# Order of the last eight units: where norms are chained and which engine scales them

## What is computed

```python
x = _layernorm(x + _L0_gnn_ref(x, adj, ...), axis=-1)
x = _layernorm(x + _L1_gnn_ref(x, adj, ...), axis=-1)
x = _layernorm(x + _L2_gnn_ref(x, adj, ...), axis=-1)
x = _layernorm(x + _L3_gnn_ref(x, adj, ...), axis=-1)
# layer 3, three times:
effects = einsum('nm,bmd->bnd', adj_matrix, v)
h = relu(concatenate([v, effects]) @ W1.T + b1)
v = h @ W2.T + b2
```

## Time and profile before

| | |
|---|---|
| median of 3 runs | 1065.37 us (1065.24 to 1068.3) |
| the profiled execution | 1068.64 us, of which the span from the first to the last instruction is 1066.8 us |
| TensorE (PE) busy | 1029.9 us, 97% of the span |
| VectorE (DVE) busy | 726.3 us, 68% |
| ScalarE (ACT) busy | 422.6 us, 40% |
| GpSimd (POOL) busy | 536.0 us, 50% |
| granted TensorE clock, mean | 0.991 of full speed |

### The profile page before, as it was taken

The page is one execution under the profiler, slowest core; times in us unless marked ns, Lnnn a source line. Parts: engine busy times, 40 slices in busy tenths (PEclk is TensorE's granted clock), DMA queues, the critical chain, the costliest instruction groups (busy, mean ns, idle before and its releaser), DMA issues.

```text
span 1066.8 us, 18773 instructions
## 1 busy us (share of the span) xinstructions
PE 1029.9 (97%) x6922; PEld 494.1 (46%) x6922; DVE 726.3 (68%) x1751; ACT 422.6 (40%) x1081; POOL 536.0 (50%) x623
## 2 busy tenths in 40 slices
PE   7979999999999999999999999999999999999994
PEld 3436444434443444344345555555554545455542
DVE  5855566577556776776674899988756776767556
ACT  3631233333434444434432564446345422132633
POOL 0001497645455866675682566677954232323310
PEclk9989999999999999999999999999999999999998
DMA  9760000000000000000010121212212100000022
GB/s 369 269 241 1 1 2 1 2 1 2 1 1 1 2 2 1 2 1 1 2 40 2 40 79 41 80 41 76 73 50 80 41 1 1 3 1 22 20 60 60
DMA packets 14658, 45.65 MB, mean 43 GB/s; under 512 B 961, under 2 KB 9281, under 8 KB 10081
## 3 DMA queue, kind: packets, MB, share of 16 engines
q1 hardware_dynamic: 14560, 44.39, 11.5%
HBM read 40.19 MB, written 4.19 MB: 42 GB/s over the span
## 4 chain that ended last, share of the span: by engine, by line
PE 82%; DVE 9%; DMA 2%; ACT 2%; POOL 2%; issue 1%; SPq 0%; POOLq 0%; ACTq 0%; DVEq 0%
PE PS L731 33%; PE PS L860 20%; PE PS L904 18%; DMA R<-at_in 2%; PE PS L716 2%; PE PS L718 2%; PE PS L717 2%; DVE T L1178 1%; DVE X L1178 1%; ACT T L1023 1%; PE PS L725 1%; PE PS L723 1%; PE PS L724 1%; DVE BW L1175 1%; DVE S L1178 1%
## 5 line engine op out<-in xcount | busy, mean ns | idle before, releaser
L731 PE MATMUL PS<-BW,S 128*128 128x512 fp8e4 x1792 | 405.2, 380 | 8.5 <-DVE T L1178 5.6
L731 PEld LDWEIGHTS PS<-BW,S 128*128 128x128 f16 x1792 | 170.0, 98 | 216.6 <-issue 18.0
L860 PE MATMUL PS<-WZ,R 64*128 64x512 f16 x1536 | 198.5, 377 | 3.1 <-ACT T L1023 3.1
L1023 ACT ACTIVATE T<-PS,SM 128x128 f32<-128x128 f32 x384 | 112.5, 365 | 207.0 <-DVE X L1178 138.0
L1726 POOL TENSOR_TENSOR T<-T 128x128 f32<-128x128 f32 (+1 forms) x192 | 126.6, 660 | 126.1 <-ACT T L1023 115.7
L1178 DVE SCALAR_TENSOR_TENSOR X<-PS,SM,X 128x128 f32<-128x128 f32 x320 | 109.8, 343 | 38.9 <-PE PS L860 38.4
L860 PEld LDWEIGHTS PS<-WZ,R 64*128 64x128 f16 x1536 | 69.3, 94 | 106.7 <-issue 25.4
L904 PE MATMUL PS<-BW,S 128*128 128x512 fp8e4 x512 | 115.4, 379 | 0.5 <-issue 0.5
L860 PE MATMUL PS<-WZ,T 64*128 64x512 f16 x768 | 103.8, 376 | 0.0
L1178 DVE SCALAR_TENSOR_TENSOR T<-PS,SM,T 128x128 f32<-128x128 f32 x256 | 88.0, 344 | 21.2 <-PE PS L860 21.2
L1726 POOL TENSOR_TENSOR S<-R,S 128x512 f16<-128x512 f32 x48 | 57.5, 1212 | 89.3 <-ACT S L1023 89.3
(11 more groups left out here) (216 smaller groups left out, 1503.8 us busy)
## 6 DMA issues: line engine op xcount, KB each, us to landing
WZ<-a_in SPq DMA_DIRECT2D x16, 1024.0 KB, 4.8
R<-at_in SPq DMA_DIRECT2D x15, 1024.0 KB, 7.0
out<-X SPq DMA_DIRECT2D x16, 256.0 KB, 2.3
X<-x_in SPq DMA_DIRECT2D x3, 1024.0 KB, 14.2
T<-w_in SPq DMA_DIRECT2D x1, 1536.0 KB, 9.4
R<-at_in SPq DMA_DIRECT2D x2, 512.0 KB, 4.6
SM<-sm_in SPq DMA_DIRECT2D x1, 520.5 KB, 16.0
X<-x_in SPq DMA_DIRECT2D x2, 256.0 KB, 4.3
```

Source lines behind the costliest of these rows:

```text
L731: m = e.matmul(o, stile(h, t, c), Bm[:, t, block(j)], start=(t == 0 and h == 0), stop=(last and t == NT - 1 and h == 1))
L860: m = e.matmul(bank(b0 + q), halves[kd][zh][r, :], WZ[r, wh, kd, block(g)], start=(i == 0), stop=(i == 8))
L1023: return e.activation(o, i, f, **kw)
```

## The change

Five things are changed in the order and in who does what:

- `var3` is split in two steps. `var3` is now VectorE's part alone, and a new step `root3` is ScalarE's square root. Each can stand at a place of its own.
- The chain of pair (3,2),(3,3): `var3` and the root stand in front of `F(2,2)`, `rs3` behind it.
- The chain of pair (2,2),(2,3): `var3` stands between the last two products, the root and `rs3` behind `V(7,6,1)`, in front of `F(3,1)`. Unit (2,3) is squared in one instruction and reduced by VectorE, between `F(3,0)` and `V(7,6,1)`.
- (3,0) and (3,1) share one chain behind `F(3,1)`, with both reductions there. `out(2,2)` and `out(2,3)` stand in front of `F(3,1)`.
- GpSimd scales (3,2) and (3,3) too.

The order that results, from V(7,5,1) on: `V(7,5,1)`, `var3(3,2)`, `root3(3,2)`, `F(2,2)`, `sq(2,2)`, `rs3(3,2)`, `out(3,2)`, `out(3,3)`, `M(7,6,0)`, `M(7,6,1)`, `V(7,6,0)`, `F(2,3)`, `M(7,6,2)`, `F(3,0)`, `sq(2,3)`, `var3(2,2)`, `M(7,6,3)`, `V(7,6,1)`, `root3(2,2)`, `rs3(2,2)`, `out(2,2)`, `out(2,3)`, `F(3,1)`, `sq(3,0)`, `sq(3,1)`, `var3(3,0)`, `root3(3,0)`, `rs3(3,0)`, `out(3,0)`, `out(3,1)`.

```diff
--- before.py
+++ after.py
@@ -217,16 +217,21 @@
     between = {}
 
     for n, s, jj, h in ((6, 1, 0, 33), (6, 1, 1, 34), (6, 4, 0, 41), (6, 4, 1, 42), (6, 5, 0, 43), (6, 5, 1, 44), (6, 6, 0, 44),
-                        (6, 6, 1, 45), (7, 1, 0, 47), (7, 1, 1, 48), (7, 4, 0, 52), (7, 4, 1, 53), (7, 5, 0, 54), (7, 5, 1, 55)):
+                        (6, 6, 1, 45), (7, 1, 0, 47), (7, 1, 1, 48), (7, 4, 0, 52), (7, 4, 1, 53)):
         on(h, ("F", *ending(n, s, jj)), ("sq", 3, *ending(n, s, jj)))
-    for n, s, h in ((6, 1, 36), (6, 4, 43), (6, 5, 46), (6, 6, 47), (7, 1, 49), (7, 4, 54), (7, 5, 56)):
+    def outs(n, s):
+        return [("out", *ending(n, s, jj)) for jj in range(2)]
+
+    for n, s, h in ((6, 1, 36), (6, 4, 43), (6, 5, 46), (6, 6, 47), (7, 1, 49)):
         u = ending(n, s, 0)
-        on(h, ("var3", *u, 2), ("rs3", *u, 2), ("out", *u), ("out", *ending(n, s, 1)))
-    u, v = ending(7, 6, 0), ending(7, 6, 1)
-    between[55] = [("F", *u)]
-    w = half[56]
-    half[56] = [("sq", 3, *u), *w[:2], ("F", *v), ("sq", 3, *v), ("var3", *u, 1), ("rs3", *u, 1), *w[2:], ("out", *u),
-                ("var3", *v, 1), ("rs3", *v, 1), ("out", *v)]
+        on(h, ("var3", *u), ("root3", *u), ("rs3", *u), *outs(n, s))
+
+    r, (u, v), (x, y) = ending(7, 4, 0), [ending(7, 5, jj) for jj in range(2)], [ending(7, 6, jj) for jj in range(2)]
+    on(54, ("var3", *r), ("root3", *r), ("F", *u), ("sq", 3, *u), ("rs3", *r), *outs(7, 4))
+    on(55, ("F", *v))
+    between[55] = [("F", *x), ("sq", 3, *v), ("var3", *u)]
+    on(56, ("root3", *u), ("rs3", *u), *outs(7, 5), ("F", *y), ("sq", 3, *x), ("sq", 3, *y), ("var3", *x), ("root3", *x),
+       ("rs3", *x), *outs(7, 6))
     for g in range(2):
         on((29, 44)[g], ("fin", g))
     for h in range(57):
@@ -617,14 +622,14 @@
                     SQPREV[x[1:]] = held.get(buf)
                     SQN[x[1:]] = len(SQN)
                     held[buf] = x[1:]
-                elif x[0] in ("var", "var3"):
+                elif x[0] in ("var", "root3"):
                     VARN[norm_key(x)] = len(VARN)
                 elif x[0] in ("rs", "rs3"):
                     RSN[norm_key(x)] = len(RSN)
 
         number_norms()
 
-        REDN = {x: n for n, x in enumerate(y for y in SQN if y[0] < 3 or not order3(*y[1:]) < 14)}
+        REDN = {x: n for n, x in enumerate(y for y in SQN if y[0] < 3 or order3(*y[1:]) > 12)}
         ORDER3 = [ending(n, s, jj) for n in (6, 7) for s in ENDS for jj in range(2)]
 
         def first_of(c, j):
@@ -633,11 +638,11 @@
 
         def by_gpsimd(c, j):
 
-            return order3(c, j) < 8 or order3(c, j) in (12, 13)
+            return order3(c, j) < 8 or 10 <= order3(c, j) < 14
 
         def summed_by_act(c, j):
 
-            return order3(c, j) < 14
+            return order3(c, j) < 13
 
         def sq_buf(L, c, j):
             return SQ[0] if L < 2 else SQC[2 * L - 4 + [y for y in SQN if y[0] == L].index((L, c, j)) % 2]
@@ -1071,12 +1076,14 @@
                         continue
                     if L == 3:
                         e.wait_ge(s_sq, SQN[L, c, j])
+                        if order3(c, j) == 15:
+                            e.wait_ge(s_red, REDN[(3, *ORDER3[13])] + 1)
                     elif SQPREV[L, c, j] is not None:
                         e.wait_ge(s_red, REDN[SQPREV[L, c, j]] + 1)
                     fn(four(sq_buf(L, c, j)), xpart(c, j), ACT.Square).then_inc(s_sq, 1)
-                elif kind in ("var", "var3"):
+                elif kind in ("var", "root3"):
                     L, c, j = (*norm_key(step), 0)[:3]
-                    m = step[3] if L == 3 else 1
+                    m = 2 if L == 3 else 1
                     e.wait_ge(s_var, VARN[norm_key(step)] + 1)
                     fn(st_part(L, c, j, 1, m), st_part(L, c, j, 2, m), ACT.Sqrt).then_inc(s_sd, 1)
                 elif kind == "row_a":
@@ -1457,18 +1464,19 @@
                     a, b = ((1 / 64 / 4096, 1e-5 / 4096), (1 / 64 / 4096, 1e-5), (1 / 64 / 4096, 1e-5))[L]
                     ts(e, st_part(L, c, 0, 2), st_part(L, c, 0, 0), a, b, ALU.mult, ALU.add).then_inc(s_var, 1)
                 elif kind == "var3":
-                    c, j, m = step[1:]
-                    if summed_by_act(c, j):
-                        e.wait_ge(s_sq, SQN[3, c, j + m - 1] + 1)
-                    else:
-                        e.wait_ge(s_red, REDN[3, c, j] + 1)
+                    c, j = step[1:]
+                    for i in (j, j + 1):
+                        if summed_by_act(c, i):
+                            e.wait_ge(s_sq, SQN[3, c, i] + 1)
+                        else:
+                            e.wait_ge(s_red, REDN[3, c, i] + 1)
                     r = order3(c, j) // 2
                     e.wait_ge(*((s_n[1], 16) if r < 2 else (s_n[3], 2 * r - 2)))
-                    ts(e, st_part(3, c, j, 2, m), st_part(3, c, j, 0, m), 1 / 64, 1e-5 * 4096, ALU.mult, ALU.add).then_inc(s_var, 1)
+                    ts(e, st_part(3, c, j, 2, 2), st_part(3, c, j, 0, 2), 1 / 64, 1e-5 * 4096, ALU.mult, ALU.add).then_inc(s_var, 1)
                 elif kind in ("rs", "rs3"):
                     L, c, j = (*norm_key(step), 0)[:3]
                     e.wait_ge(s_sd, VARN[norm_key(step)] + 1)
-                    s0, s1, s2 = (st_part(L, c, j, k, step[3] if L == 3 else 1) for k in range(3))
+                    s0, s1, s2 = (st_part(L, c, j, k, 2 if L == 3 else 1) for k in range(3))
                     fc(e.reciprocal(s1, s1))
                     fc(e.tensor_tensor(s0, s1, s1, ALU.mult))
                     fc(e.tensor_tensor(s0, s0, s2, ALU.mult))
```

## The result

The changed kernel takes 1064.47 us (median of 22 runs, 1061.13 to 1066.32), the kernel before 1067.42 us (22 runs, 1063.62 to 1068.75). The ratio of the runs is 0.9971, 95% interval 0.9964 to 0.9978, which is 3.1 us less (2.3 to 3.8). I had forecast 1062.0 us with a range up to 1064.2: the time lies 0.3 us outside it. The kernel before itself stands 2.05 us above the 1065.37 us of the three runs that I had started from.

What follows compares the result with a forecast made beforehand. TensorE, busy 97% of the span, was taken as the bound, with gains only where it waits or has finished. 1.36 + 0.95 + 1.19 - 0.1 - 0.05 = 3.35 us off the 1065.37 us median gave 1062.0 us, range 1061.2 to 1064.2.

Steps and rivals of the forecast that it cites:

- the transfers: Last two output transfers, now starting 0.80 us apart instead of 2.09: the second waits, costing 0.1 us (0 to 0.5).
- Part 1: Root of pair (3,2),(3,3) before the squares of (2,2), scalings on GpSimd: F(3,0) starts on TensorE 1.36 us earlier.
- hold by GpSimd: High half of V(7,6,0) held until GpSimd's second scaling of (3,2),(3,3) is over: costs 0.48 us.
- the second rival: More than one instruction held by GpSimd, or root still after the squares: 1063.1 us, 1064.2 with two holds; chance 0.20.
- Part 2: Unit (2,3) reduced on VectorE between F(3,0) and V(7,6,1): costs nothing, with 1.25 us of cover.
- Part 3: Behind V(7,6,1) only rs3(2,2) stands before F(3,1) on VectorE: its lag behind TensorE falls from 1.82 to 0.87, gaining 0.95 us.
- Part 4: One chain of norms for (3,0),(3,1) behind F(3,1), instead of two chains and scalings: 1.19 us gained.
- the added wait: One more semaphore for var3 to wait for: 0.05 us (0 to 0.1) on the last chain, nothing for earlier pairs.
- 0.12 us of room: var3(3,0) starts 0.12 us after GpSimd's scalings of (2,2),(2,3) end, so nothing is held, barely.
- the third: VectorE's wait for the root becomes one for V(7,6,0)'s ReLU, TensorE gains nothing there: gain 2.0 us, 1063.4 us; chance 0.06.

Runs made afterwards that it cites:

- the ungated version: Changed kernel with F(3,0) behind M(7,6,3), VectorE scaling (3,2),(3,3), GpSimd scaling (2,2),(2,3) at once: 1064.39 us (one execution), stretch from V(7,5,1) to last scaling 19.45 us.

## Why the prediction missed

**The miss is in the level, not in the change.** The step that failed is the last of the sum: "So I subtract from the median". It took 1065.37 us, from three runs that span 3 us, as the level of the kernel before, and its range allowed 0.13 us for it. Over 22 runs, these three among them, that level is 1067.42 us, and 19 and 15 further runs gave 1067.74 and 1067.68. Seven of the 22 lie below 1066 us, and two of the first three were of these: the draw was bad luck, but taking it as the level to 0.13 us was the mistake. The forecast difference of 3.35 us stands against 2.95 us between the medians, 3.1 us (2.3 to 3.8) by the ratio, and 3.27 us in the profiles (3.43 in the stretch less 0.16 in the transfers). The prediction saw that the profiled execution was 3.27 us above the median and that the terms don't depend on it; it didn't draw the conclusion that the level itself was unsure by as much. With 1067.42 the same sum gives 1064.07 us, 0.4 us off. (The lower end of the range, 1061.2, comes to 1061.3 by its own terms; nothing hangs on it.) That most of the spread comes in ahead of layer 0's weight stage (3.7 us, against 0.8 us from there to `V(7,5,1)`) is shown for the eleven profiled executions; that the three runs were low for the same reason is argued, as they have no profiles, and both profiled executions of before belong to the upper level. What made them low stays open.

**Part 1** was forecast at 1.36 us, measured 1.47 (`F(3,0)` 8.99 us after `V(7,5,1)` before, 7.52 us after). The 0.11 us more: `var3` pushed `F(2,2)` back by 0.07 us, not 0.20 (1042.01 and 1042.08); `F(2,2)` needs nothing of it. All behind it, the squares and the ReLU, came 0.12 to 0.13 us earlier than worked out. The high half of `V(7,6,0)` starts 1.98 us earlier and gives 0.50 of them back. This hold by GpSimd was forecast at 0.48 us. It is shown by two experiments, of which one moves only GpSimd's start; the ungated version shows that the second rival, two holds in a row, is real where two scalings meet two such instructions.

**Part 2** cost nothing, as forecast. In the changed kernel VectorE still waits 1.10 us for the ReLU of `V(7,6,1)`.

**Part 3**: 0.95 forecast, 0.95 measured (1.82 less 0.87), 0.94 when undone.

**Part 4**: 1.19 forecast, 1.01 measured (6.68 us from `F(3,1)` to the end of the last scaling before, 5.67 after). The step "From `F(3,1)` to `var3(3,0)` it is 2.42 us as before" was wrong: it is 2.60 us, of which 0.06 are the added wait, for which the sum had its own 0.05, and 0.12 come with the need for the reduction's result, a term that the prediction didn't have. Its 0.12 us of room against GpSimd's scalings grew by just that, and nothing was held.

**The transfers**: 0.1 forecast, 0.16 measured (2.83 less 2.67, as near as the spans, given to 0.1 us, allow). That the sum of 3.35 came within 0.08 us of 3.27 is in part luck: 0.11 us too little in part 1 stand against 0.13 too much in part 4 and its wait, and 0.06 in the transfers.

Of the rivals none happened as a whole. The first half of the third did, VectorE's wait for the root became one for the ReLU, but a shorter one, and TensorE gained. The 3.1 us by the ratio fall just short of the 3.2 us from which the prediction counted "faster", so it is "same" by its own measure (given 0.44 against 0.52); the interval holds both.

## What to carry to other kernels

Look at what stands between a wait and the instruction that another engine needs: moving the wait's cause ahead (here a root queued behind eight squares) lets all that is behind it start earlier. Before moving work to GpSimd, look at what VectorE does at that moment: the scalings cost nothing beside multiply-adds out of PSUM, and 0.5 to 1.35 us beside the high and lower halves. Where VectorE waited anyway, the same work was free there. And when a forecast is of a difference, say the difference, and find out first how far the level spreads. The profile of the end alone told terms of 0.1 us apart that 22 runs could not.

## What the runs showed of the hardware

- TensorE's wait before `F(3,1)` was 2.06 us in nine of the eleven profiles. In seven of these its clock was at full speed (2.4 GHz) for the twelve matmuls behind it, in two it fell to half (1.2 GHz) during them, at a cost of 0.11 and 0.44 us. Behind the one wait of 2.73 us (GpSimd at once) it stayed at full speed. A wait of the same length can be free or not.
- Executions of practically the same code reached layer 0's weight stage at 119.5 to 123.2 us. The earliest had a wait of 3.33 us and a clock of 0.96 of full speed between 62 and 102 us, the first of before 5.59 us and 0.85 to 0.88; it came 2.9 us later.
- A GpSimd scaling in progress held VectorE's high half (0.43 us alone) to 0.93 or 1.05 us and the lower half (0.69 us alone) to 1.42 us.
- `var3` on VectorE, an instruction of 0.17 us, started 0.60 us behind a reduction of 0.69 us that it did not need, 0.72 us behind one that it needed, and 0.78 us with one more semaphore to wait for that was fulfilled by then.
